# Part of the shared expert moves into the distance pass; row norms come from a TensorE product; routing runs every three units

## The reference

```
1  x += cross attention (16 heads of 64) from xn into ctx
2  x += shared expert + routed experts:
     shared(xn) = (silu(xn @ sg.T) * (xn @ su.T)) @ sd.T          sg, su: 512 x 256
     scores = sigmoid(xn @ router.T) over 16 experts in 4 groups; the best 2 groups, of these the best 4 experts
     routed(xn) = sum over the 4 of weight * expert(xn)             experts with 64 hidden values
3  D[i,j] = sqrt(max(|ctx_i|^2 + |xn_j|^2 - 2 ctx_i.xn_j, 0)) per sequence, time-warping path through D,
     x += rows of ctx gathered along the path
4  x += quantised linear, depthwise convolution, silu, quantised linear
```

## Time and profile before

| | |
|---|---|
| median of 3 runs (lowest to highest) | 3097.36 us (3094.02 to 3100.95) |
| profiled execution | 3095.66 us, span 3093.7 us |
| PE busy, share of the span | 2696.2 us, 87% |
| DVE, ACT, POOL busy | 2198.3 (71%), 1755.8 (57%), 1984.8 (64%) |

### The profile page before, as it was taken

How to read it: one execution, slowest core, us unless ns; L and a number is a source line. 1 busy time by engine, 2 the same in 40 slices (tenths; PEclk the granted TensorE clock), 3 DMA queues, 4 the chain that set the end, 5 groups by cost and what they waited for, 6 DMA issues and landing times. The chain is left out here.

```text
span 3093.7 us, 61611 instructions
## 1 busy us (share of the span) xinstructions
PE 2696.2 (87%) x20082; PEld 2325.6 (75%) x20085; DVE 2198.3 (71%) x5038; ACT 1755.8 (57%) x4605; POOL 1984.8 (64%) x2046
## 2 busy tenths in 40 slices
PE   6999999999999999999996999899994533189897
PEld 5888888888888888888886888788884521057675
DVE  5767676777777676776765888555554668889997
ACT  5666666666666666666663333233332335099997
POOL 4888888888888888888884666500004800078896
PEclk9999999999999999999996999999997755599999
DMA  8665656665666666666563000111113870001111
GB/s 219 114 114 109 114 110 112 111 116 108 115 116 113 112 110 113 110 114 110 110 110 98 29 27 29 41 53 57 56 57 100 194 143 1 15 28 42 49 35 42
DMA packets 710936, 274.99 MB, mean 89 GB/s; under 512 B 606393, under 2 KB 685857, under 8 KB 710626
## 3 DMA queue, kind: packets, MB, share of 16 engines
q1 hardware_dynamic: 704194, 253.19, 40.6%
q0 software_dynamic: 6432, 17.86, 1.9%
HBM read 104.32 MB, written 32.39 MB: 44 GB/s over the span
## 5 line engine op out<-in xcount | busy, mean ns | idle before, releaser
L844 POOL COPY attention_probT<-attention_planesT 128x1024 uint16<-128x1024 uint16 x512 | 676.1, 1367 | 179.7 <-PE attention_turns L422 106.2
L529 ACT ACTIVATE attention_prob<-attention_turns,attention_neg_max 128x256 f32<-128x256 f32 x1024 | 467.6, 481 | 228.7 <-DVE attention_neg_max L682 222.2
L835 POOL COPY attention_planes<-attention_prob 128x1024 uint16<-128x1024 uint16 x512 | 527.0, 1060 | 20.4 <-ACT attention_prob L529 20.4
L682 DVE TENSOR_REDUCE attention_neg_max<-attention_turns 128x2 f32<-128x512 f32 x512 | 318.0, 683 | 175.4 <-PE attention_turns L407 175.1
L383 PE MATMUL attention_turns<-kv_hi,wkv 128*128 128x512 f32 x1024 | 374.4, 406 | 0.0
L351 PE MATMUL attention_turns<-wkv,kv_hi 128*128 128x512 f32 x1024 | 315.5, 389 | 1.9 <-ACT attention_prob L529 1.9
L1808 POOL DMA_INDIRECT far_routed_rows<-rows_out,back_places x64 | 70.1, 1095 | 371.7 <-POOLq L1619 354.6
L422 PE MATMUL attention_turns<-attention_probT,attention_v 128*64 128x128 f32 x4096 | 255.9, 278 | 1.9 <-issue 1.9
L518 ACT COPY attention_v<-attention_turns 128x512 f32<-128x512 f32 x256 | 150.4, 589 | 187.1 <-PE attention_turns L351 186.8
L698 DVE TENSOR_TENSOR attention_turns<-attention_turns,attention_attT_lo 128x512 f32<-128x512 f32 x128 | 140.0, 1094 | 147.5 <-DMA attention_attT_lo<-inverse_rows 145.4
L422 PEld LDWEIGHTS attention_turns<-attention_probT,attention_v 128*64 128x64 f32 x4096 | 224.8, 138 | 19.5 <-issue 2.8
(11 more groups left out here) (361 smaller groups left out, 8058.7 us busy)
## 6 DMA issues: line engine op xcount, KB each, us to landing
attention_attT_lo<-inverse_rows SPq DMA_DIRECT2D x256, 128.0 KB, 3.0
experts_rows<-rows_in SPq DMA_DIRECT2D x69, 132.0 KB, 2.1
rows_out<-experts_down_raw SPq DMA_DIRECT2D x69, 128.0 KB
attention_ctx<-in_ctx SPq DMA_DIRECT2D x32, 256.0 KB, 3.3
attention_planesT<-attention_planes SPq DMA_TRANSPOSE x512, 3.2
far_ctxT<-in_ctxT SPq DMA_DIRECT2D x32, 256.0 KB
weights_ctx<-in_ctx SPq DMA_DIRECT2D x16, 512.0 KB, 3.8
out<-conv_x_out SPq DMA_DIRECT2D x15, 512.0 KB, 2.8
```

Of the source, the lines that this page charges most:

```text
L529: made = act.activation(prob[n % 2][:, h, :], bank_of("s", 2 * n + e)[:, m * 256:(m + 1) * 256], ACT.Exp, bias=neg_max[:, n % 2, 2 * e + m ...
L682: made = dve.tensor_reduce(neg_max[:, n % 2, 2 * e:2 * e + 2], bank_of("s", 2 * n + e)[:, :].rearrange("p (h c) -> p h c", h=2), AX.X, ALU ...
L835: pool.tensor_copy(planes[n % 2][:, g, :, :], words.rearrange("p (c b) -> p b c", b=2)).then_inc(planes_made, 1)
L844: pool.tensor_copy(words.rearrange("p (c b) -> p b c", b=2), planesT[:, g, :, :]).then_inc(joined, 1)
```

## The change

1. Groups 3, 7 and 11 (`LATE`) are taken out of the shared stage; `SHARED_ORDER` puts them last. 52 units (`NF`) stay, and 12 run in the distance pass with buffers of their own (one bank each for gate and up). Group 3's turned and split x is made at the end of the shared stage (`second_xT`), those of groups 7 and 11 in two extra slots of the distance pass.
2. Routing is laid out three units a group (`PER_ENTRY`, `AFTER_TURN`), with the steps counted from the unit of the transposes. Both halves of x are transposed at once, into the banks `misc` and `aux`; the bank `aux` is shared with the ranks, so `turn` waits for `places_made`. The normalisation moves from DVE to ACT with a scale and a shift that POOL makes. `route_picks` loses two multiplications by the group mask, and its second part becomes `route_classes` in the next unit. The pads are scattered in three pairs.
3. In the distance pass the row norms are put on the diagonal of a tile (`spread_norm`, ACT, four copies of the identity with a scale), and a product with a tile of ones adds them to the products in PSUM; `clamp` adds the context's norm as its bias. The trip through DRAM and `add_norms` go.
4. `ctxT` is stored in the order in which it is loaded, one load a group instead of two. There is one pair of banks `turns` instead of two, and DVE copies the turned x of the slot just before, ahead of adding the next group.

```diff
+    LATE = range(3, NG - 1, 4)
+    FIRST = [g for g in range(NG) if g not in LATE]
+    SHARED_ORDER = [*FIRST, *LATE]
+    NF = STILES * len(FIRST)
...
-            u = STILES * g
...
-            return {"measure": u - 7, "norm": u - 6, "turn0": u - 5, "turn1": u - 4, "scores": u - 3,
-                    "groups": u - 2, "picks": u - 1, "ranks": u + 1, "scatter": u + 2}[kind]
+        PER_ENTRY = 3
+        AFTER_TURN = {"measure": -2, "norm": -1, "turn": 0, "scores": 1, "groups": 2, "picks": 3, "classes": 4, "ranks": 5,
+                      "places": 6, "scatter": 6}
...
+        def turn_unit(e):
+            return PER_ENTRY * (e - 1) if e < NG else NF - STILES
...
+            def turn(e):
+                pe.wait_ge(normed, e)
+                pe.wait_ge(tanh_made, e)
+                if ranked_before(turn_unit(e)):
+                    pe.wait_ge(places_made, ranked_before(turn_unit(e)))
...
+            def normalise(e):
+                act.wait_ge(rstd_made, e)
...
+                    made = act.activation(xr[e % ROWS][:, i, 0:DIM], x_all[:, GB * group_of(e) + i, :], ACT.Identity,
+                                          scale=rstd[:, i:i + 1], bias=shift[:, i:i + 1])
...
+        TURNS = [("far", i) for i in range(NG)]
+        for j in range(len(FIRST) + 1, NG):
+            TURNS.insert(2 + 5 * (j - len(FIRST) - 1), ("inputs", j))
...
+            for q in range(SLOTS + 1):
+                if q < SLOTS:
+                    if unit_at(q) is not None:
+                        up_gate(unit_at(q))
+                    turn(q)
+                if 1 <= q <= NL:
+                    down_proj(NF + q - 1)
+                if q and is_far(q - 1):
+                    multiply(fars(q - 1))
...
+                pe.matmul(far_ps[s][:, :], ones[:, :], spread[s][:, :], start=True, stop=False, skip_group_check=True)
...
+            for q in range(SLOTS + 2):
+                if 0 <= q - 1 < SLOTS:
+                    if is_far(q - 1):
+                        copy_far(q - 1)
+                        spread_norm(fars(q - 1))
+                    else:
+                        high_x(q - 1)
+                if q < SLOTS:
+                    if unit_at(q) is not None:
+                        gate_silu(unit_at(q))
+                    normalise(q)
+                    if unit_at(q) is not None:
+                        high_hidden(unit_at(q))
+                if 0 <= q - 2 and is_far(q - 2):
+                    clamp(fars(q - 2))
...
+            for q in range(SLOTS):
+                inverse_std(q)
+                if unit_at(q) is not None:
+                    low_hidden(unit_at(q))
+                if is_far(q) and fars(q) + YGS < NG:
+                    gather(fars(q) + YGS)
```

More of the change, by code:

```diff
@@ L1324, in act_program @@
                 high_weight(n)
-            for n in range(N):
+            normalise(1)
+            for n in range(NF):
                 gate_silu(n)
@@ L1521, in dve_program @@
             route_groups(0)
-            for n in range(N + 2):
-                if n < N:
+            for n in range(NF + 2):
+                if due("places", n) is not None:
+                    find_places(due("places", n))
+                if n < NF:
                     weigh_hidden(n)
```

668 lines of the change are left out of this document (373 added, 295 removed).

## The result

The changed kernel takes 3128.34 us (median of 4 runs, 3125.43 to 3130.43), the kernel before on the same chip 3098.98 us. The ratio is 1.0102, 95% interval 1.009 to 1.0115: slower by 1.0%. Its profiled execution took 3126.52 us, 30.9 more than the 3095.66 of the profiled execution before.

What follows compares the result with a forecast made beforehand. The prediction took TensorE (PE) to bound the shared stage and a GpSimd (POOL) chain the distance pass. -54.6+81.3 = +26.7 on 3095.66 gave 3122.4, and 1.7 more for the median 3123 us; own case 3103 to 3140, 61%.

Steps and rivals of the forecast that it cites:

- the stage: Shared-expert stage, up to the first sorted tile: forecast -54.6 us (-40 to -68) from 347.0, with twelve units leaving giving -50.8.
- the pass: Distance pass, where the twelve units go: forecast +81.3 us, with bounds of +65 and +119.
- Start: First eight units of the shared stage: reordered routing and normalisation on ACT cut the loss from 21.6 to 10.6, -11 us (0 to -18).
- Pauses: Shared stage: PE stalls since the POOL and ACT chain takes 16.9 us a round against PE's 15.3; +9 us (0 to 20).
- walk: Shared stage: count through fourteen rounds, units 6 to 48, with 2.1 us of slack used up and refilled; gave +9 us.
- Tail: End of the shared stage: earlier placement and paired pads, less 4.5 us of stalls, -2.6; separately +0.8 for group 3's extra transposes.
- Slots with a unit: Distance pass: POOL waits 2.7 us for ACT ahead of the low half; 11.1 us bare, 12.0 forecast a plain slot.
- the stretch: Distance pass: added per unit slot, 0.68 us kept from today's chain above POOL's own 7.05, and 0.3 for late silu.
- The ring: Distance pass, slots 13 to 17: small operations, normalisation, transposes, copy, adding and measuring follow one another, 9.9 us against 7.73.
- POOL's own work as the only bound: Rival, distance pass: unit slots cost 9.0 us, the pass +29, the whole 3072 us; chance 7%.
- PE at 1.2 GHz all through: Rival, distance pass unit slots: pauses bring PE's clock down and it stays down, pass +119, whole 3162 us; chance 10%.
- the stage kept more than 305 us: Shared stage: a sign that the prediction was wrong; it expected about 292 us in the profile after.

Runs made afterwards that it cites:

- stay: Changed kernel with all 64 units kept in the shared stage, four units a routing round, pads scattered behind the last unit: 3142.71 us, 1.0154 of the kernel before.
- sh_places: Changed kernel with VectorE finding a group's places ahead of the next group's masks in the shared stage: 3127.55 us, 1.0097 of the kernel before.
- sh_scatter4: Changed kernel with POOL's scatters one unit later in the shared stage and a fourth buffer of normalised rows: 3144.97 us, 1.0154 of the kernel before.
- far_copy_last: Changed kernel with VectorE's squared norms and copy of turned x moved behind the next group's adding and measuring in the pass: 3112.19 us, 1.005 of before.
- stay_copy_last: The stay kernel with VectorE's copy of turned x moved behind adding and measuring the next group: 3108.82 us, 1.0044 of the kernel before.
- far_gather_first: Changed kernel with POOL's gathers issued ahead of the low half of the hidden rows in the pass: 3125.92 us, 1.0089 of the kernel before.
- far_both: Changed kernel with VectorE's copy behind adding and measuring, and POOL's gathers ahead of the low half: 3089.63 us, 0.9974 of the kernel before.

## Why the prediction was right, and where it was off

The time (3128.34 against 3123) and the sign were right, in part because two misses of opposite sign cancelled: the stage gave back 14.3 us less than forecast, and the pass, with the sorted tiles ahead of it, cost 7.0+3.1 = 10.1 us less. That the sum came within 5 us is to that extent luck. The 14.3 are 5.0 at the start, 7.7 in the pauses and 1.6 at the tail.

- **Start: mis-sized.** PE's gate product of the thirteenth unit starts 1731.97-1657.91 = 74.1 us into the stage. Before it was 1736.69-1656.65 = 80.0, from the rows below: -6.0, where the prediction had -11. PE's idle time ahead of that unit fell only from 11.4 to 7.3 us. The longest pause left is the one of 4.79 at the second transposes, for group 0's places; it was foreseen (5). The scores of one group more also fall ahead of the mark now, about 1.7 us of PE.

```profile
1731.97 0.51 PE L1153 MATMUL experts_gate_up<-second_xT_hi,gate_up 128*128 128x512 f32 x1
...
1931.20 0.48 PE L1153 MATMUL experts_gate_up<-first_xT_hi,gate_up 128*128 128x512 f32 x1
```
```profile
1736.69 0.47 PE L1126 MATMUL experts_gate_up<-experts_xT_hi,gate_up 128*128 128x512 f32 x1
...
1970.04 0.40 PE L1126 MATMUL experts_gate_up<-experts_xT_hi,gate_up 128*128 128x512 f32 x1
```

- **Pauses: mis-sized.** Twelve rounds after that mark, in which 36 units ran (49th unit at 1931.20) instead of 48 (61st at 1970.04), took 199.2 instead of 233.4 us. Less the 50.8 of the units that is +16.7, where the prediction had +9; 14.1 of it is PE idle, and before PE had no idle time at all there. Its walk let the slack be "used up and refilled"; it is refilled, but only once in four rounds, behind each group whose units moved away, and the pauses are 1.2 to 1.9 us in the other three. Two things were wrong in the walk. It took a loop that carries one group in 16.9 us as the limit, where stay has the pause with a round of 21.9, and it did not contain VectorE, of which it only said that its work "fits". VectorE's places end as late as ACT's rows, and 1.0 us of its chain is standing still beside POOL: in each of the nine rounds with a pause one operation of the masks took 1.2 to 1.3 us instead of 0.22. That each chain holds the pause when the other is shortened is shown by sh_places and by sh_scatter4. That removing both would give the pauses back is not shown: every kernel that tried brought a longer wait with it.
- **Tail: mis-sized.** From those marks to the first sorted tile it is 33.4 instead of 33.6 us, -0.2 against -2.6+0.8. PE waits 1.34 for ACT's rows ahead of the last transposes, 1.82 ahead of the counts for ACT's copy of x and 0.35 at a down product, 3.5 of the 4.5 us that I had counted, so the gain in placing and padding was smaller than forecast. No run takes this apart.
- **Slots with a unit.** POOL's wait of 2.7 us was seen to the tenth in the rows. The seven plain slots took 80.4 us instead of 84.0. Four of them (1, 3, 6, 9) took 11.0 to 11.3, near the bare 11.1; in the other three (5, 10, 11), 11.9, one gather that began within VectorE's addition took 1.93 to 1.95 us instead of 0.95. So the stretch that I had spread as 0.68+0.3 over all of them is one gather in some. Slot 0 took 11.3 (12.5). Slots 4 and 8 took 25.9 (25.8), which is luck: 13.9 and 12.0 where I had 12.9 for each; slot 12 took 13.3 (13.3), the input slots 22.3 (23.4), the slots without a unit 38.4 (39.6).
- **The ring.** 9.9 us was right to the tenth (9.88 in slots 13 and 16, 9.88 or 9.89 in eight of the fifteen of stay), and far_copy_last and stay_copy_last show its cause. The slots of 9.0 among them are the 9.0 that I had for PE at full clock: their transposes take 1.1 us and not 1.97. What I did not see is that the ring is a second limit right behind POOL's wait in the unit slots, 9.3 us in two of them and 11.3 where VectorE's addition is held (far_gather_first).
- **Rivals.** POOL's own work as the only bound, in which a slot with a unit takes 9.0 us, is what far_both comes near (8.4 to 9.5 in its plain slots). PE at 1.2 GHz all through did not come (granted clock 0.84 in the pass), but one transpose still takes 417 to 421 ns (median) in the changed kernel and 273 in far_both. I had said that I would be wrong if the stage kept more than 305 us: it kept 306.7, and that step was.

## What to carry to other kernels

When work is put into a stage whose engines are each half idle, write down the order of every engine for one slot and follow each ring through all of them. Here a copy placed ahead of the next group's measuring, and a low half ahead of the gathers, cost 39 us together, while undoing one gave 16 us or 2.4: undoing the low half alone would have acquitted it. In a stage where one engine is full, a step moved on a second engine needs three checks before it is called free: the buffer that it holds longer, what queues behind it, and which operations of VectorE it now runs beside.

## What the runs showed of the hardware

In these traces VectorE operations on two SBUF operands were held beside POOL's halves, and did not get in between two of these that follow closely: 0.19 us became 5.53 and 0.22 became 5.04, each ending with the last of three POOL operations (2.50+2.37 and 2.51+2.41 us). The kernel before has it too: its product of scores and group mask (L1417, 128x64) has a median of 910 ns and ends 0.1 us after POOL's low half in group after group. An operation with one tensor in SBUF can be held as well: the first of the masks, 193 ns in the median of the changed kernel, took 1.17 us beside POOL's 1.30. The operation of 5.53 us began 0.6 us ahead of the first of the three, while a scatter was being issued; another of 0.19 us just ahead of it ran beside the same scatter at full speed, and why the one passed and not the other stays open. Search operations were not held: a match-and-replace at 1806.25 in the changed kernel took 0.16 us beside POOL's 1.29, and all 64 of that line took 156 to 167 ns. Gathers and additions met in one direction only: a gather that began within an addition of 1.22 us took up to 1.96 us instead of 0.95 (2424.72 in the kernel before), while no addition of routed rows in the kernels before and after took over 1.27 us.

```profile
1798.57 1.17 DVE L1419 TENSOR_SCALAR experts_score<-experts_small 128x64 f32<-128x64 f32 x1
...
1806.25 0.16 DVE L1447 MATCH_REPLACE8 experts_marked<-experts_top,experts_masked 128x16 f32<-128x16 f32 x1
```
```profile
1798.38 1.30 POOL L1625 TENSOR_TENSOR experts_hidden_lo<-experts_weighed,experts_hidden_hi 128x512 fp32r<-128x512 f32 x1
...
1805.81 1.29 POOL L1625 TENSOR_TENSOR experts_hidden_lo<-experts_weighed,experts_hidden_hi 128x512 fp32r<-128x512 f32 x1 [2.81 <-ACT experts_hidden_hi L1323]
```
